# A third buffer of normalised sums, weights' parts a tile ahead, and another order where the experts begin

## What is computed

```python
seq = (layernorm(x) @ W_seq).reshape(N, H, DH)
scores = leaky_relu(score1[:, :, None] + score2[:, None, :], 0.2) + (1 - adj) * MASK_VAL
hidden = einsum('hij,jhd->ihd', softmax(scores), seq).reshape(N, D)
x = x + elu(hidden @ W_out + b_out)                      # the projection

xf = layernorm(x)                                        # 2048 x 512
lat = xf @ fc1_w.T                                       # 2048 x 256
shared = relu2(xf @ up_w.T) @ down_w.T                   # 512 -> 2048 -> 512
# routing: 2 of 8 experts for each token; tokens sorted by expert
he = relu2(xs @ w1[e].T) @ w2[e].T                       # for the rows of expert e
x = x + scatter_add(he * score) @ fc2_w.T + shared
```

## Time and profile before

| | us |
|---|---|
| median of 3 runs (lowest, highest) | 1034.56 (1034.47, 1037.38) |
| the profiled execution's own time | 1036.99 |
| its span, first to last instruction | 1035.2 |
| PE busy | 992.7 |
| DVE busy | 793.9 |
| ACT busy | 664.1 |
| POOL busy | 263.8 |

### The profile page before, as it was taken

How to read it: one execution, slowest core, us unless ns; L and a number is a source line. 1 busy time by engine, 2 the same in 40 slices (tenths; PEclk the granted TensorE clock), 3 DMA queues, 4 the chain that set the end, 5 groups by cost and what they waited for, 6 DMA issues and landing times.

```text
span 1035.2 us, 27169 instructions
## 1 busy us (share of the span) xinstructions
PE 992.7 (96%) x11243; PEld 881.7 (85%) x11243; DVE 793.9 (77%) x1175; ACT 664.1 (64%) x995; POOL 263.8 (25%) x312
## 2 busy tenths in 40 slices
PE   7998899999999999998988999999999989999998
PEld 6877899999999999997767888888888877778887
DVE  6789999999999999964986333457766579866554
ACT  3479999999898989714775343344455556655431
POOL 3112233344433343453431000000263000006500
PEclk9999999999999999999999999999999999999999
DMA  9931111111111111803763000110163124453242
GB/s 245 107 66 41 63 44 43 63 44 43 44 45 62 43 43 44 271 22 110 234 221 135 1 1 1 23 60 1 51 213 103 56 92 129 125 179 89 91 129 101
DMA packets 53600, 89.99 MB, mean 87 GB/s; under 512 B 5904, under 2 KB 30096, under 8 KB 52976
## 3 DMA queue, kind: packets, MB, share of 16 engines
q1 hardware_dynamic: 43104, 67.26, 19.6%
q0 software_dynamic: 7296, 12.59, 6.8%
q10 hardware_dynamic: 3088, 8.49, 2.6%
HBM read 74.82 MB, written 26.08 MB: 97 GB/s over the span
## 4 chain that ended last, share of the span: by engine, by line
PE 43%; DVE 4%; DMA 2%; ACT 2%; issue 1%; POOL 1%; SPq 0%; DVEq 0%; ACTq 0%; POOLq 0%
PE bank L1365 17%; PE bank L1832 16%; PE bank L1909 2%; DMA xs<-sorted_latent_rows 2%; PE bank L691 1%; PE bank L1860 1%; PE bank L1861 1%; PE bank L1863 1%; PE bank L1817 1%; DMA xr<-in_x 1%; PE bank L1815 1%; DVE hid L1156 1%; DVE hid L1159 1%; PE bank L1853 1%; PE bank L1814 1%
## 5 line engine op out<-in xcount | busy, mean ns | idle before, releaser
L753 ACT ACTIVATE arena<-arena 128x1024 fp8e4<-128x1024 f32 x320 | 336.9, 1135 | 2.4 <-ACT arena L745 1.4
L1007 PE MATMUL bank<-arena 128*128 128x132 f16 x4096 | 283.5, 220 | 12.1 <-DVE arena L853 6.4
L1007 PEld LDWEIGHTS bank<-arena 128*128 128x128 fp8e4 x4096 | 244.4, 97 | 13.9 <-DVE arena L853 7.4
L1365 PE MATMUL bank<-xt,up_parts 128*128 128x512 f32 x768 | 187.9, 394 | 2.1 <-DVE up_parts L1349 2.1
L1832 PE MATMUL bank<-down_parts,h_parts 128*128 128x512 f32 x768 | 184.5, 389 | 0.0
L1011 PE MATMUL bank<-arena 128*128 128x66 f16 x4096 | 172.4, 195 | 0.0
L1365 PEld LDWEIGHTS bank<-xt,up_parts 128*128 128x128 f32 x768 | 143.4, 189 | 31.4 <-issue 2.1
L1832 PEld LDWEIGHTS bank<-down_parts,h_parts 128*128 128x128 f32 x768 | 143.9, 188 | 30.0 <-issue 0.2
L824 DVE TENSOR_SCALAR arena<-arena 128x1024 uint8<-128x1024 f32 x192 | 169.3, 948 | 0.0
L1011 PEld LDWEIGHTS bank<-arena 128*128 128x128 fp8e4 x4096 | 153.5, 98 | 0.0
L1339 DVE TENSOR_TENSOR relu_sb<-relu_sb 128x512 f32<-128x512 f32 x64 | 44.3, 692 | 119.9 <-ACT relu_sb L1314 119.8
(11 more groups left out here) (244 smaller groups left out, 1381.2 us busy)
## 6 DMA issues: line engine op xcount, KB each, us to landing
arena<-s_rows SPq DMA_DIRECT2D x32, 512.0 KB, 3.7
sorted_latent_rows<-zeros SPq DMA_DIRECT2D x1, 4992.0 KB, 18.2
xs<-sorted_latent_rows SPq DMA_DIRECT2D x39, 128.0 KB, 2.1
sorted_expert_rows<-expert_y SPq DMA_DIRECT2D x39, 128.0 KB, 1.7
arena<-in_adjT POOLq DMA_DIRECT2D x8, 512.0 KB, 27.1
xr<-in_x SPq DMA_DIRECT2D x16, 256.0 KB, 4.7
x_rows<-hid SPq DMA_DIRECT2D x16, 256.0 KB, 4.2
up_sb<-in_upT ACTq DMA_DIRECT2D x4, 1024.0 KB, 5.5
```

The lines of the kernel that those rows point to most:

```text
L753: last = nc.scalar.activation(m8[:, k, j, :], s1b[:, k % 2, :], ACT.Sigmoid, bias=bias_now[:, k % 2, j:j + 1], scale=STEEP, saturate=False)
L1007: last = nc.tensor.matmul(o, m8[:, k, j, i * P:(i + 1) * P], vs[:, b, j, :], start=(j == 0), stop=(j == T - 1))
L1365: last = nc.tensor.matmul(bank[6 + s % 2][:, :], sa[:, s % 2, a, k, :], xt[c][:, b, k, :], start=(i == 0), stop=(i == len(mm) - 1))
```

## The change

Four edits, none of which adds or removes work:

1. `hn` gets a third buffer, in the place of the bias row `bout_sb`. POOL normalises one tile further ahead: in step 3 it runs `normalise` for tiles 3 and 4, then in step t for tile t+1, each time ahead of `root(t - 3)`.
2. In step 14 instead of 15, and behind the ELU instead of ahead of it, ACT makes the first two high parts of up. DVE's low parts stay in step 15.
3. Where the experts begin, DVE makes the low half of the second sorted tile between the second and the third eviction; the low parts of up and down for later steps move into the experts' loop, to its tile 4, and ACT's high part of down to tile 3.
4. `xs` gets a fourth buffer.

```diff
-        hn = place("hn", 28928, [2, D])
+        hn = [place(f"hn{b}", o, [D]) for b, o in enumerate((28928, 29440, 28032))]
...
         def normalise(pool, t):
             pool.wait_ge(rden_ready, 1 if t < IT else 2)
-            if t >= 2:
-                pool.wait_ge(ht_in_psum, t - 1)
-            nc.gpsimd.tensor_tensor(hn[:, t % 2, :].rearrange("p (h d) -> p h d", h=H), hid[:, t, :, 0:DH],
+            if t == 2:
+                pool.wait_ge(wo_low, 1)
+            if t >= 3:
+                pool.wait_ge(ht_in_psum, t - 2)
+            nc.gpsimd.tensor_tensor(hn[t % 3].rearrange("p (h d) -> p h d", h=H), hid[:, t, :, 0:DH],
...
             for t in range(T):
                 if 2 <= t + 1 < T:
                     copy_h(act, t + 1)
-                if t == T - 1:
+                elu_parts(t)
+                if t == T - 2:
                     act.wait_ge(up_loaded, 16 * KD)
                     act.wait_ge(x1_stored, 16 * EARLY)
                     act.wait_ge(xn2_ready, EARLY)
                     high_a(act, 0)
                     high_a(act, 1)
-                elu_parts(t)
...
             for t in range(T + 3):
-                if 3 <= t < T:
-                    normalise(pool, t)
+                if t == 3:
+                    normalise(pool, 3)
+                if 3 <= t < T - 1:
+                    normalise(pool, t + 1)
                 if t >= 3:
                     root(t - 3)
...
-        xs = place("xs", 41216, [3, LAT])
+        xs = [place(f"xs{b}", o, [LAT]) for b, o in enumerate((41216, 41472, 41728, 8192))]
...
-                    if i >= 3:
-                        sp.wait_ge(xs_in_psum, i - 2)
-                    sp.dma_start(xs[:, i % 3, :], xs_dram[i * P:(i + 1) * P, :]).then_inc(xs_loaded[i % 3], 16)
+                    if i >= 4:
+                        sp.wait_ge(xs_in_psum, i - 3)
+                    sp.dma_start(xs[i % 4], xs_dram[i * P:(i + 1) * P, :]).then_inc(xs_loaded[i % 4], 16)
...
                     if s + 2 < STEPS:
                         high_a(act, s + 2)
+                    if s == 3 * FS + 1:
+                        return
                     high_b(act, s)
...
                 for i in range(-2, TILES):
                     if i + 3 < TILES:
                         high_xs(i + 3)
+                    if i == 3:
+                        high_b(act, 3 * FS + 1)
...
                     low_h(dve, s - 1)
                     if s == 3 * FS + 1:
                         low_xs(0)
-                    if s % FS == 1:
+                        evict(2, range(2))
+                        low_xs(1)
+                        evict(2, range(2, TT))
+                    elif s % FS == 1:
                         evict(s // FS - 1)
...
+                    if s == 3 * FS + 1:
+                        return
                     if s + 2 < STEPS:
                         low_a(dve, s + 2)
                     low_b(dve, s)
...
                 for i in range(-2, TILES):
-                    if i + 3 < TILES:
+                    if -2 < i and i + 3 < TILES:
                         low_xs(i + 3)
+                    if i == 4:
+                        low_a(dve, 3 * FS + 3)
+                        low_b(dve, 3 * FS + 1)
```

More of the change, by code:

```diff
@@ L679, in transpose_h @@
             for k in range(KD):
-                last = nc.tensor.transpose(bank[6 + t % 2][:, k * P:(k + 1) * P], hn[:, t % 2, k * P:(k + 1) * P], ident2)
+                last = nc.tensor.transpose(bank[6 + t % 2][:, k * P:(k + 1) * P], hn[t % 3][:, k * P:(k + 1) * P], ident2)
             last.then_inc(ht_in_psum, 1)
@@ L1294, in build @@
         pair_high, pair_ready = sem("pair_high"), sem("pair_ready")
-        xs_loaded = [sem(f"xs_loaded{b}") for b in range(3)]
+        xs_loaded = [sem(f"xs_loaded{b}") for b in range(4)]
         y_stored = [sem(f"y_stored{b}") for b in range(3)]
@@ L1557, in step, with evict @@
                     dve.wait_ge(dve_step, steps[0])
-                def evict(c):
+                def evict(c, tiles=range(TT)):
                     dve.wait_ge(x1_loaded[c % 2], 16 * (c // 2 + 1))
-                    for t in range(TT):
+                    for t in tiles:
                         if t < TT - 1:
@@ L1848, in transpose_xs @@
                 def transpose_xs(j):
-                    pe.wait_ge(xs_loaded[j % 3], 16 * (j // 3 + 1))
+                    pe.wait_ge(xs_loaded[j % 4], 16 * (j // 4 + 1))
                     if j >= 1:
@@ L1852, in transpose_xs @@
                     for k in range(KL):
-                        last = nc.tensor.transpose(T1[:, k * P:(k + 1) * P], xs[:, j % 3, k * P:(k + 1) * P], ident3)
+                        last = nc.tensor.transpose(T1[:, k * P:(k + 1) * P], xs[j % 4][:, k * P:(k + 1) * P], ident3)
                     last.then_inc(xs_in_psum, 1)
```

## The result

| | before | changed |
|---|---|---|
| median of 5 runs (lowest, highest), us | 1034.56 (1033.33, 1037.38) | 1028.39 (1027.70, 1030.34) |
| ratio of paired runs, 95% interval | | 0.9923 (0.9905 to 0.9941) |
| the same, measured once more with 6 runs | | 0.9929 (0.9905 to 0.9953) |
| the profiled execution: own time, span | 1036.99, 1035.2 | 1028.39, 1026.6 |

By the two ratios the change makes the kernel faster by 7.3 to 8.0 us. The medians of the two series lie 6.2 and 7.2 us apart. The forecast was 5.1.

The account below looks back on a forecast made before the run. PE, busy 96% of the span, bounds the kernel, with DVE at 4.38 us a projection tile next behind the removed waits. Projection 4.59 plus experts 0.5 make 5.1 us off 1034.56, so 1029.5 us; range 1026.8 to 1032.8.

Parts of the forecast that it names:

- Start: Projection's first tiles: PE's 2.17 us wait for tile 4's normalise goes; tile 3's variance row comes 1.69 us earlier.
- Steady tiles: Projection, variance rows of tiles 3 to 10 (v3 to v10): seven tiles at 4.38 us each, saving 0.55 us.
- Tiles 11 and 12: Projection, v10 to v12: `xr` wait of 0.4 us instead of 1.0, tile 12 without collision; saves 1.20 us.
- First weights' parts: Projection's end: DVE's wait for ACT's first high parts of up goes; saves 1.15 us.
- Experts: Where the experts begin: first `expert_y` 1.7 us sooner, 1.2 us paid back at tile 4; net 0.5 us.
- Fourth buffer: Experts' loop: the fourth `xs` buffer gives 0, since SP's order, not a free buffer, issues the loads.
- the rival that gave it 3.5 us: Experts' loop: the fourth `xs` buffer removes DVE's 3.5 us; 8.6 us saved, 1026.0 us; chance 0.04.
- the projection's four steps: Start, steady tiles, tiles 11 and 12, and first weights' parts, together 4.59 us saved in the projection.

Follow-up runs that it names:

- the repeat: The changed kernel measured and profiled once more, unchanged; ratio to the kernel before 0.9929.
- `after_split`: The changed kernel with the first 2 MB of `down_sb` loaded in four loads of 512 KB instead of one; ratio to the kernel before 0.9943.
- `hn3_alone`: The kernel before with only the third buffer of normalised sums and POOL's normalise one tile further ahead; ratio 0.9941.
- `xs4_alone`: The kernel before with only the fourth `xs` buffer; ratio 0.9994.
- `lead6_xs3`: The changed kernel with each `xs` load one store earlier in SP's order, but with three `xs` buffers; ratio to the kernel before 0.9917.
- three later edits: On the changed kernel: normalise held to the residual's second add, `xs` loads one store earlier, first 2 MB of `down_sb` in four loads; together 1021.40 us.

## Why the prediction was too small

The sign, the places and most terms were right; the size was not. The measured 0.9923 of 1034.56 is 1026.6, just below the range's low end of 1026.8; the median of the changed runs, 1028.39, lies inside it. The step that failed is the one that put the tensor engine's clock at the same level in both kernels (7 below). Two terms of the sum were also mis-sized (1 and 3).

1. *Start, 1.69 forecast.* From tile 2 to 3 the first profile gives 5.55 - 4.57 = 0.98, the repeat 5.55 - 3.14 = 2.41. The step failed where it said that the second add would meet normalise 7. In the first profile `xr` of tile 3 landed 0.70 late and the first add ran into normalise (1.30 us at 489.69). In the repeat it landed in time, and the adds came first:

```profile
489.05 0.68 DVE L1160 SCALAR_TENSOR_TENSOR hid<-xr,pos 128x512 f32<-128x512 f32 x1
```

```profile
489.15 0.63 POOL L1140 TENSOR_TENSOR std<-mv,rstd 128x1 f32<-128x1 f32 x1
489.85 0.65 POOL L1142 TENSOR_TENSOR std<-std,halves 128x1 f32<-128x1 f32 x1
490.46 1.05 POOL L667 TENSOR_TENSOR hn<-hid,rden 128x512 f32<-128x512 f32 x1
```

   The two small products of the root took 0.63 and 0.65 instead of 0.19 us: it was they that waited for DVE, and normalise came behind the adds. That is the rule that I cited (SBUF — State Buffer, "SBUF: two separate sides" in the Trainium skill) with POOL as the loser; the forecast had applied it to normalise alone.
2. *Steady tiles, 0.55 forecast.* v3 to v10 took 523.41 - 492.70 = 30.71 us instead of 31.21: 0.50. Right.
3. *Tiles 11 and 12, 1.20 forecast.* 532.37 - 523.41 = 8.96 instead of 9.64: 0.68. Normalise 15 left tile 12 as forecast (3.66). The wait for `xr` was mis-sized: the forecast took 0.4, the wait row says 1.55, the upper end. Behind so long a wait the second add no longer met a normalise (0.69 at 527.04 instead of 1.42), so the tile lost 0.92. `after_split` shows the cause of the wait.
4. *First weights' parts, 1.15 forecast.* v12 to v15 fell from 12.2 to 11.0: 1.25. The size is right, but `hn3_alone` shows that 0.9 of it comes with the third buffer.
5. *Experts, 0.5 forecast.* 1.79 gained (1.7 forecast), 1.29 paid back (1.2): net 0.50. Right.
6. *Fourth buffer, 0.* Right in both orders; the rival that gave it 3.5 us fell by `xs4_alone` and `lead6_xs3`.
7. *Not in the sum:* the granted clock. The sum took each product at the full clock in both kernels, and so put this term at nothing without reading it. That failed: edit 1 removed a stretch behind which the clock fell in 3 of 5 profiles, and edit 3 one behind which it fell in 1 of 7. On the average of runs this is worth 1.2 to 2.2 us by the three estimates above. With the steps at 3.9 us (start of the first profile) or 5.1 (start of the repeat and five others) it makes 5.1 to 7.3 us. The intervals of the two measurements begin at 6.1 and 4.9; their middles, 8.0 and 7.3, lie above this or at its end, so up to 3 us of the gain has no shown cause. The 3.2 us of `xs` waits between the two profiles are chance: the sums are 3.2 to 8.9 us in the kernels with the old order, 3.1 to 7.6 with the new one.

In the repeat the projection's four steps make 2.41 + 0.32 + 0.61 + 1.25 = 4.6, the forecast's 4.59. That is luck: the start gave 0.7 us more than forecast, steps 2 and 3 gave 0.8 less.

The third buffer's 6.1 us alone against 3.0 in its profile, and 3.6 against 1.1 for edit 2, are not fully explained: by their mean clocks of 0.9960 and 0.9962, beside 0.9945 for before in the same series, the clock's share is at most 1.5 and 1.7 us. Edit 2 removes none of the idle stretches, so why its runs had fewer falls is open as well. What decides, behind the same idle stretch, whether the clock falls in a given execution stays open too.

## What to carry to other kernels

- An idle stretch of PE costs more than its length if the clock falls behind it. Read the granted clock window by window next to every long wait of PE (here 1.4 to 2.3 us), and count its price (here 1.57 us where it falls) for a change that removes the wait. Compare the length of the same products in two profiles before believing in a difference.
- Where two engines exclude one another, look for a time in the other's cycle that doesn't need the port, and hold the instruction there. One added wait gave 0.5 us a tile.
- One profile is one draw of the late loads. Before a loop's waits are put into a sum or explained, ask which of them the program's order fixes and which only happen.
- Compare the parts' ratios with the whole's. Here four parts measured alone add up to more than the change, and three later edits that seemed worth nothing alone gave 8 us together: a ratio open by 1.5 to 2.5 us can't size a step of 1 us, the rows can.

## What the runs showed of the hardware

- The granted clock fell behind idle stretches of 1.85 to 2.3 us with products on both sides, in some executions and not in others. The Trainium skill (TensorE: Matmul & The Clock Gate, "HAM oscillation — how this bites in real kernels") tells of a kernel in which each wait for a load throttles the products behind it; the waits here are single and shorter, and in 10 of 18 chances at the first two stretches it happened all the same.
- About every eighth `xs` load of the experts' loop landed late. In the profile of before the loads issued at 858.99, 875.51 and 891.84 took 3.2, 3.0 and 3.8 us, in that of the changed kernel those at 853.57, 869.34 and 885.48 took 2.5, 2.9 and 2.7, and most others 2.1. PE wants them after 2.65. One store of lead hides all of them.
